# Two-layer transformer on one Trainium2 core: row-tiled maxima in layer 0's attention, one values block per unit in layer 1's

## The chip, the core and the metric

The kernel runs on one core of one Trainium2 chip. The core has five engines with a queue of their own each: PE (matmuls; its weight loads are listed as PEld), DVE (vector), ACT (scalar), POOL (GpSimd) and SP, which here only issues DMAs. They meet through semaphores. PE multiplies out of SBUF into PSUM, which has eight banks of 128 partitions x 512 fp32 values. The metric is the device time of one execution in microseconds. The kernel before takes 1522.89 us, the median of three runs (1521.58 to 1523.54).

## What is computed

Two layers, each an attention block and a feed-forward block with adaptive layer norms around them. The change touches the two softmax attentions. Layer 0's, cut to what matters (batch 2, sequence 1024, 16 query heads in 4 groups of 4 that share a key and value head, head dimension 64):

```python
q = (hidden_states @ Wq.T).reshape(B, S, NUM_HEADS, HEAD_DIM).transpose(0, 2, 1, 3)
k = (hidden_states @ Wk.T).reshape(B, S, NUM_KV_HEADS, HEAD_DIM).transpose(0, 2, 1, 3)
v = (hidden_states @ Wv.T).reshape(B, S, NUM_KV_HEADS, HEAD_DIM).transpose(0, 2, 1, 3)
...
scores = jnp.einsum('bhqd,bhkd->bhqk', q, k) * scale
scores = scores + causal[None, None]
probs = jax.nn.softmax(scores, axis=-1)
out = jnp.einsum('bhqk,bhkd->bhqd', probs, v)
return out.transpose(0, 2, 1, 3).reshape(B, S, NUM_HEADS * HEAD_DIM) @ Wo.T
```

The second attention, in the feed-forward block of layer 1, has the same form over the same 2048 tokens, with a head dimension of 8.

## The kernel before

The program is a chain of stages with a barrier between them. `stage_attention64` (layer 0) and `stage_attention8` (layer 1) work in the same way. A group g is one key head with its four query heads in one batch; there are 8. A group has 12 units, each 128 keys against up to 512 queries: four for the first half of the queries, eight for the second. On the diagonal a unit is only 384, 256 or 128 queries wide (`unit_lo`). For a unit PE makes transposed scores, ACT takes their exponential, POOL clears what lies above the diagonal, and two units later (`LAG`) PE multiplies the result with the values (`values`), out of weights of 32 columns on the four column quarters of the array.

The exponential needs each query's maximum before the scores, since it goes into the score matmul as a row (row 64 of `qB`, written by SP from `mT`). So a group's maxima are made while the group before is in its units: as max jobs, scores the other way round (queries on the partitions, keys along the bank), each reduced by DVE. Their matmuls stand in PE's queue as fills behind the scores.

Layer 0. Queries and keys are split: `proj` jobs (L500) give q and k from doubled weight columns, ACT rounds them to the high part (L708, L711), DVE subtracts it for the low part (L619, L624). A query head lies in `qA` with its high part on partitions 0 to 63 and its low part on 64 to 127; `kH` holds the key's high part twice. A score is two matmuls: L548 over 128 partitions, and L549 over 65 (the key's low part with `qB`, a copy of the query's high part that SP makes by DMA, plus the row of maxima). A max job (L510) is one matmul of 128 partitions for each head; with a key width of 128, 256, 384 or 512 a job takes 4, 2, 1 or 1 heads side by side in a bank, and a mask matmul in bf16 (L516) lies on the diagonal. There are 38 max jobs to a group, 22 with a mask. All jobs (proj, max, turn, fin) pass in one order through three banks (`JOB_BANKS`): job i waits until DVE is done with job i-3 (`w_free`). DVE takes them in the same order (`take`), with the copies of finished outputs (L655, L656), the reciprocals and the normalisation (L669) in fixed places between. A turn job (L522) transposes the maxima; fin (L528) is the output projection. `spread_over` lays the jobs over the units by weight (proj 3, others 1) and unit width, `parts` lays a unit's jobs and its three rounds of values over its score pieces. Where a unit opens an output (`opens`) no values stand behind its first score piece.

Layer 1. The 64 rows of a head's operands hold all split terms, so two heads lie on the halves of the array's rows (`row_tile`), as two matmuls into two banks. Scores (L983) go to three banks (`SCORE_BANKS`), so a score waits for the exponential of the score three before. A unit of 512 or 384 queries has four score jobs, a narrower one two. The max jobs (L956, masks L967 on the same row halves) use two pairs of banks. The values (L1009) are one bank.

```python
between = n >= LAG and len(jobs) == 4 and (n - LAG) % NU not in (0, 4)
```

Where `between` holds, a unit's values block stands between its second and its third score, otherwise behind the fourth. It holds for units 0, 1, 4, 5, 7, 8 and 9 of a group.

## Time and profile before

| | us |
|---|---|
| median of three runs | 1522.89 |
| the profiled execution, its time | 1521.91 |
| its span, first to last instruction | 1520.2 |
| layer 0's attention in it | about 39 to 646 |
| layer 1's attention in it | about 1021 to 1317 |
| PE busy, whole span | 1325.6 (87%) |
| DVE busy, whole span | 969.0 (64%) |
| ACT busy, whole span | 696.5 (46%) |

A row of the timeline has the start, the time to the end of the last instruction of the row, the engine, the line, the operation, what it writes and reads, and how many instructions are merged. Matmuls overlap: a matmul's recorded duration holds the filling and draining of the array, so what one costs the queue is the difference between its end and the end of the matmul before it. Where rows are added up here, that difference is meant. A values matmul of the order below is two instructions in the trace.

### The profile page before, as it was taken

How to read it: one execution, taken by the hardware profiler on the slowest of the kernel's cores; microseconds unless marked ns; L12 is line 12 of the kernel's file. 1: busy time of each engine (PE TensorE's matmuls, PEld its weight loads, DVE VectorE, ACT ScalarE, POOL GpSimd, SP SyncE). 2: the span in 40 equal slices, each digit the busy share in tenths (PEclk: the TensorE clock that was granted, in tenths of full speed). 3: DMA queues.
4: the chain of work that ended last, by engine and by line, in shares of the span. 5: the costliest groups of instructions: out<-in, count | busy, mean ns of one | idle time of the engine just before them, and what ended most of it. 6: DMA issues, size and time to landing. Idle time of an engine off the chain costs nothing. (4 is left out here: it accounts for less than half of the span.)

```text
span 1520.2 us, 21410 instructions
## 1 busy us (share of the span) xinstructions
PE 1325.6 (87%) x7772; PEld 762.8 (50%) x7772; DVE 969.0 (64%) x1750; ACT 696.5 (46%) x1319; POOL 112.6 (7%) x155
## 2 busy tenths in 40 slices
PE   4689999999999999868999967337989888889998
PEld 3344444444444444346888845313334333256886
DVE  4556545454546462177999966748767655357998
ACT  2242434333333433244666654412665556525664
POOL 0000000101010101000000000302111111020000
PEclk9799999999999999959999979656999888868999
DMA  3101202020201110006676610041212210102221
GB/s 104 40 15 34 49 15 63 8 58 15 52 15 43 29 29 16 14 15 144 146 154 153 146 24 1 2 100 54 47 48 49 53 40 20 43 21 79 78 102 28
DMA packets 51475, 81.61 MB, mean 54 GB/s; under 512 B 16748, under 2 KB 34452, under 8 KB 47444
## 3 DMA queue, kind: packets, MB, share of 16 engines
q1 hardware_dynamic: 51004, 79.40, 21.2%
q10 hardware_dynamic: 384, 1.05, 0.6%
q8 instruction: 55, 0.90, 0.2%
q14 instruction: 32, 0.26, 0.1%
HBM read 63.75 MB, written 5.68 MB: 46 GB/s over the span
## 5 line engine op out<-in xcount | busy, mean ns | idle before, releaser
L1345 PE MATMUL ps<-qA 128*128 128x512 f32 x960 | 252.3, 399 | 15.3 <-POOL qA L1455 10.9
L634 DVE TENSOR_REDUCE mraw<-ps 128x1 f32<-128x512 f32 (+3 forms) x304 | 186.8, 656 | 108.7 <-PE ps L516 60.2
L736 ACT ACTIVATE shared<-ps 128x512 f32<-128x512 f32 (+1 forms) x216 | 121.3, 566 | 261.4 <-PE ps L549 259.8
L1062 DVE TENSOR_REDUCE mraw<-ps 128x2 f32<-128x1024 f32 (+3 forms) x160 | 173.5, 1114 | 78.0 <-PE ps L967 52.3
L1117 ACT ACTIVATE shared<-ps 128x512 f32<-128x512 f32 (+2 forms) x320 | 155.7, 560 | 136.6 <-PE ps L983 136.0
L1345 PEld LDWEIGHTS ps<-qA 128*128 128x128 f32 x960 | 182.5, 192 | 62.9 <-POOL qA L1455 12.3
L548 PE MATMUL ps<-qA,kH 128*128 128x512 f32 (+3 forms) x384 | 165.9, 442 | 6.1 <-DMA qB<-mT 5.8
L548 PEld LDWEIGHTS ps<-qA,kH 128*128 128x128 f32 x384 | 72.9, 190 | 150.7 <-issue 62.6
L1409 ACT CAST qA<-shared 128x512 fp32r<-128x512 f32 x160 | 99.3, 621 | 88.6 <-DVE shared L1547 87.0
L1357 PE MATMUL ps<-qA,kH 128*128 128x512 f32 x480 | 136.3, 393 | 4.0 <-DVE qA L1471 4.0
L549 PE MATMUL ps<-qB,kL 65*128 65x512 f32 (+3 forms) x384 | 130.5, 350 | 0.0
L510 PE MATMUL ps<-kH,qA 128*128 128x512 f32 (+3 forms) x384 | 116.6, 369 | 9.4 <-DVE qA L624 7.8
L1471 DVE TENSOR_TENSOR qA<-shared,qA 128x512 fp32r<-128x512 f32 x160 | 110.0, 688 | 7.0 <-ACT qA L1409 2.0
L573 PE MATMUL ps<-shared 128*32 128x512 f32 (+3 forms) x1024 | 107.3, 509 | 0.0
L1547 DVE TENSOR_TENSOR shared<-shared 128x512 f32<-128x512 f32 x156 | 106.8, 685 | 0.0
L1357 PEld LDWEIGHTS ps<-qA,kH 128*128 128x128 f32 x480 | 90.2, 189 | 24.9 <-DVE qA L1471 6.1
L1009 PE MATMUL ps<-shared,VP 128*32 128x512 f32 (+3 forms) x768 | 93.9, 566 | 0.8 <-ACT oU L1104 0.4
L983 PE MATMUL ps<-qA,kH 64*128 64x512 f32 (+3 forms) x288 | 81.0, 461 | 14.9 <-ACT shared L1117 8.8
L956 PE MATMUL ps<-kL,qA 64*128 64x512 f32 (+3 forms) x288 | 70.3, 458 | 25.3 <-DMA kH<-qB 16.6
L736 ACT ACTIVATE rB<-ps 128x512 f32<-128x512 f32 x88 | 52.2, 599 | 87.7 <-PE ps L549 87.4
L510 PEld LDWEIGHTS ps<-kH,qA 128*128 128x128 f32 x384 | 69.8, 195 | 27.4 <-DVE qA L624 10.2
L983 PEld LDWEIGHTS ps<-qA,kH 64*128 64x128 f32 x288 | 37.7, 207 | 84.8 <-ACT shared L1117 57.8
(247 smaller groups left out, 1755.2 us busy)
## 6 DMA issues: line engine op xcount, KB each, us to landing
shared<-comb SPq DMA_DIRECT2D x92, 256.0 KB, 4.3
qB<-qA SPq DMA_DIRECT2D x16, 512.0 KB, 4.8
rB<-a0rec_dram SPq DMA_DIRECT2D x60, 128.0 KB, 2.8
shared<-comb SPq DMA_DIRECT2D x7, 1024.0 KB, 4.4
rB<-a1rec_dram SPq DMA_DIRECT2D x28, 128.0 KB, 2.7
e0wUp<-in_w SPq DMA_DIRECT2D x48, 64.0 KB, 4.5
qA<-q_split SPq DMA_DIRECT2D x24, 128.0 KB
q_split<-qA SPq DMA_DIRECT2D x4, 512.0 KB
```

Of the source, the lines that this page charges most:

```text
L510: ins = nc.tensor.matmul(bank[:, i * width:(i + 1) * width], k.qA[par][:, h0 + i, qt * P:(qt + 1) * P], k.kH[par][:, ch * 512:ch * 512 + w ...
L548: nc.tensor.matmul(out, k.kH[par][:, keys], k.qA[par][:, h, cols], start=True, stop=False)
L549: ins = nc.tensor.matmul(out, k.kL[par][0:hd + 1, keys], k.qB[par][0:hd + 1, h, cols], start=False, stop=True)
L573: nc.tensor.matmul(O[r][CT * at:CT * (at + 1), lo:512], v, probs(n)[:, 2 * r + i, lo:512], start=first, stop=last, skip_group_check=True)
L634: nc.vector.tensor_reduce(out[:, h0:h0 + n_h, qt % 4], src, AX, ALU.max).then_inc(w_free, 1)
L736: nc.scalar.activation(probs(n)[:, hs[0]:hs[-1] + 1, lo:512], src, ACT.Exp, scale=scale)\
L983: ins = nc.tensor.matmul(score_bank(s)[:, slot * w:(slot + 1) * w], kOne[g % 3][rows, kt * P:(kt + 1) * P], Q[g % 3][rows, h // 2, qc * 51 ...
L1062: nc.vector.tensor_reduce(out[:, :, js[0]:js[-1] + 1, qt % 4], src, AX, ALU.max).then_inc(x_free, 1)
L1117: nc.scalar.activation(dst, src, ACT.Exp, scale=scale).then_inc(p_done, 1)
L1345: ins = nc.tensor.matmul(bank[0:M, :], w[par][:, at:at + M], h[:, cols], start=(r == 0), stop=(r == 2))
L1357: ins = nc.tensor.matmul(acc(ch), w[par][:, m * D:(m + 1) * D], f[0:M, i % 2, :], start=(opens and r == 0), stop=(closing and r == 2), ski ...
L1471: nc.vector.tensor_tensor(fL[0:M, i % 2, :], k.hid[0:M, i % 2, :], fH[0:M, i % 2, :].bitcast(F32), ALU.subtract).then_inc(a_full, 1)
```

## The change

In layer 0 a query head of even number keeps its high part on partitions 0 to 63, and one of odd number has it on 64 to 127, the low part in the other half. ACT and DVE write them so (the same instructions, other partitions), and the DMA that copies the high parts to `qB` becomes two, one for the even and one for the odd heads. A max job now has heads of one parity and uses the high parts alone, 64 partitions; jobs come in pairs (`maxima`), an even and an odd one with alternating matmuls on the two halves of the array's rows, into two banks. Behind them stand both mask matmuls, still over 128 partitions. A pair waits until DVE has freed the bank of its second job. With key widths up to 256 a job holds two heads, otherwise one: 40 max jobs to a group in 20 pairs, 12 pairs with masks. A pair has weight 2 and is one fill. DVE reduces each job by itself.

In layer 1 `between` goes: the values always stand behind the unit's last score and fills.

```diff
--- before.py
+++ after.py
@@ -392,29 +392,31 @@
         out = []
         for qt in range(4 * qc, 4 * qc + 4):
             for ch in range(qc + 1):
-                n = 512 // keys_in(qt, ch)
-                out += [(qt, ch, h, n) for h in range(0, REP, n)]
+                if keys_in(qt, ch) <= 256:
+                    out += [(qt, ch, i, (i, i + 2)) for i in range(2)]
+                else:
+                    out += [(qt, ch, h % 2, (h,)) for h in range(REP)]
...
-        out += some[0:3] + [("proj", g, 1, 1)] + some[3:6] + [("proj", g, 1, 2)] + some[6:]
-        return out + more[0:3] + [("turn", g, 0, 0)] + more[3:]
+        out += some[0:2] + [("proj", g, 1, 1)] + some[2:4] + [("proj", g, 1, 2)] + some[4:]
+        return out + more[0:2] + [("turn", g, 0, 0)] + more[2:]
...
-        weights = [3 if job[0] == "proj" else 1 for job in jobs]
+        weights = [{"proj": 3, "max": 2}.get(job[0], 1) for job in jobs]
...
-        due[n] = list(range(len(JOBS), len(JOBS) + len(plan[n])))
-        JOBS += plan[n]
+        due[n] = []
+        for kind, g, qc, j in plan[n]:
+            both = [(kind, g, qc, j), (kind, g, qc, j + 1)] if kind == "max" else [(kind, g, qc, j)]
+            due[n].append(tuple(range(len(JOBS), len(JOBS) + len(both))))
+            JOBS += both
...
+                def maxima(pair):
+                    kind, g, qc, j = JOBS[pair[0]]
+                    par = g % 2
+                    if pair[1] >= JOB_BANKS:
+                        pe.wait_ge(w_free, pair[1] - JOB_BANKS + 1)
+                    if j == 0:
+                        pe.wait_ge(w_free, index["proj", g, qc, U - 1] + 1)
+                    qt, ch, _, evens = MAXES[qc][j]
+                    width = keys_in(qt, ch)
+                    diagonal = ch * 512 + width == (qt + 1) * P
+                    n_h = len(evens)
+                    for slot, h in enumerate(evens):
+                        for i in range(2):
+                            half = slice(i * hd, (i + 1) * hd)
+                            ins = nc.tensor.matmul(k.bank(pair[i] % JOB_BANKS)[:, slot * width:(slot + 1) * width],
+                                                   k.qA[par][half, h + i, qt * P:(qt + 1) * P],
+                                                   k.kH[par][half, ch * 512:ch * 512 + width], start=(slot == 0),
+                                                   stop=not diagonal, skip_group_check=True)
+                            if not diagonal and slot == n_h - 1:
+                                ins.then_inc(w_full, 1)
+                    if diagonal:
+                        for i in range(2):
+                            ends = k.bank(pair[i] % JOB_BANKS)[:, 0:n_h * width]\
+                                .rearrange("p (h w) -> p h w", w=width)[:, :, width - P:width]
+                            nc.tensor.matmul(ends, k.ident_bf[:, :], k.masks[:, 1:2, :].broadcast_to((P, n_h, P)),
+                                             start=False, stop=True, skip_group_check=True).then_inc(w_full, 1)
...
-                        pe.wait_ge(qb_ld[qc], 16 * (g + 1))
+                        pe.wait_ge(qb_ld[qc], 32 * (g + 1))
...
-                                ins = nc.vector.tensor_tensor(k.qA[par][hd:2 * hd, h, cols],
+                                ins = nc.vector.tensor_tensor(k.qA[par][(1 - i) * hd:(2 - i) * hd, h, cols],
                                                               bank[i * hd:(i + 1) * hd, :],
-                                                              k.qA[par][0:hd, h, cols].bitcast(F32), ALU.subtract)
+                                                              k.qA[par][i * hd:(i + 1) * hd, h, cols].bitcast(F32),
+                                                              ALU.subtract)
...
-                            ins = nc.scalar.copy(k.qA[par][0:hd, 2 * (j - 1) + i, cols], bank[i * hd:(i + 1) * hd, :])
+                            half = slice(i * hd, (i + 1) * hd)
+                            ins = nc.scalar.copy(k.qA[par][half, 2 * (j - 1) + i, cols], bank[half, :])
...
-                    sp.dma_start(k.qB[g % 2][0:hd, :, cols].bitcast(F32), k.qA[g % 2][0:hd, :, cols].bitcast(F32))\
-                        .then_inc(qb_ld[qc], 16)
+                    for i in range(2):
+                        sp.dma_start(k.qB[g % 2][0:hd, i::2, cols].bitcast(F32),
+                                     k.qA[g % 2][i * hd:(i + 1) * hd, i::2, cols].bitcast(F32)).then_inc(qb_ld[qc], 16)
...
@@ -1016,7 +1043,6 @@
                 for n in range(STEPS + LAG):
                     jobs = score_jobs(n) if n < STEPS else []
                     fills = list(due.get(n, []))
-                    between = n >= LAG and len(jobs) == 4 and (n - LAG) % NU not in (0, 4)
                     for at in range(max(len(jobs), 1)):
                         if at < len(jobs):
                             score_job(n, first_score[n] + at, *jobs[at])
@@ -1025,9 +1051,7 @@
                             for idx in fills[:share]:
                                 max_job(idx)
                             fills = fills[share:]
-                        if at == 1 and between:
-                            values(n - LAG)
-                    if n >= LAG and not between:
+                    if n >= LAG:
```

The order on PE from the last slot of a group's unit 5 (units are counted from 0) over the first two slots of its unit 6, layer 0 (L548 and L549 are scores, L510 maxima, L516 masks, L573 a round of values). Before:

```order
L548 MATMUL ps<-qA,kH 128x512
L549 MATMUL ps<-qB,kL 128x512
L510 MATMUL ps<-kH,qA 128x512
L516 MATMUL ps<-masks,ident_bf 128x128
L548 MATMUL ps<-qA,kH 128x512
L549 MATMUL ps<-qB,kL 128x512
L510 MATMUL ps<-kH,qA 128x512
L516 MATMUL ps<-masks,ident_bf 128x128
L548 MATMUL ps<-qA,kH 128x512
L549 MATMUL ps<-qB,kL 128x512
L510 MATMUL ps<-kH,qA 128x512 x2
L573 MATMUL ps<-shared 32x512 x4
```

Now (L568 and L569 are the scores, L510 the maxima, L520 the masks, L593 values):

```order
L568 MATMUL ps<-qA,kH 128x512
L569 MATMUL ps<-qB,kL 128x512
L510 MATMUL ps<-kH,qA 128x512 x2
L520 MATMUL ps<-masks,ident_bf 128x128 x2
L568 MATMUL ps<-qA,kH 128x512
L569 MATMUL ps<-qB,kL 128x512
L510 MATMUL ps<-kH,qA 128x512 x2
L568 MATMUL ps<-qA,kH 128x512
L569 MATMUL ps<-qB,kL 128x512
L510 MATMUL ps<-kH,qA 128x512 x2
L593 MATMUL ps<-shared 32x512 x4
```

The four max jobs of these three slots were one, one and two matmuls of full height. Now there are six, a pair of half height in each slot, and between the pair of one slot and that of the next stand only two score matmuls.

DVE at the same place (L624 the low parts of queries, L669 the normalisation, L634 the reductions, L655 and L656 the copies out of the output banks, L605 the fold of the maxima). Before:

```order
L669 TENSOR_TENSOR oU<-oU,rB 128x2x512
L634 TENSOR_REDUCE mraw<-ps 128x1 x4
L655 COPY S<-ps 128x512
L656 COPY oU<-ps 128x512
L634 TENSOR_REDUCE mraw<-ps 128x1
L605 COPY mmax<-mraw 128x16
L634 TENSOR_REDUCE mraw<-ps 128x1 x3
```

Now:

```order
L690 TENSOR_TENSOR oU<-oU,rB 128x2x512
L644 TENSOR_TENSOR qA<-ps,qA 64x512 x2
L655 TENSOR_REDUCE mraw<-ps 128x1 x4
L625 COPY mmax<-mraw 128x16
L676 COPY S<-ps 128x512
L677 COPY oU<-ps 128x512
L655 TENSOR_REDUCE mraw<-ps 128x1 x4
```

One projection's low parts now stand behind the normalisation, and behind the copies stand four reductions, those of unit 6's first two pairs, where before some of unit 6's came behind one and a fold.

Layer 1's attention on PE, from the block that is due in unit 5 to the block that is due in unit 7 (group 3) (L983 scores, L956 and L967 maxima and masks, L1009 values). Before:

```order
L1009 MATMUL ps<-shared,VP 32x128 x4
L983 MATMUL ps<-qA,kH 128x512 x2
L956 MATMUL ps<-kL,qA 128x256 x4
L967 MATMUL ps<-halves 128x2x128 x4
L983 MATMUL ps<-qA,kH 128x512 x2
L956 MATMUL ps<-kL,qA 128x512 x2
L983 MATMUL ps<-qA,kH 128x512 x2
L1009 MATMUL ps<-shared,VP 32x512 x4
L983 MATMUL ps<-qA,kH 128x512 x2
L956 MATMUL ps<-kL,qA 128x512 x2
L1009 MATMUL ps<-shared,VP 32x512 x4
```

Now (L1010 scores, L983 and L994 maxima and masks, L1036 values):

```order
L1036 MATMUL ps<-shared,VP 32x128 x4
L1010 MATMUL ps<-qA,kH 128x512 x2
L983 MATMUL ps<-kL,qA 128x512 x2
L1010 MATMUL ps<-qA,kH 128x512 x2
L1036 MATMUL ps<-shared,VP 32x512 x4
L1010 MATMUL ps<-qA,kH 128x512 x2
L983 MATMUL ps<-kL,qA 128x512 x2
L1010 MATMUL ps<-qA,kH 128x512 x2
L983 MATMUL ps<-kL,qA 128x384 x2
L994 MATMUL ps<-halves 128x128 x4
L1036 MATMUL ps<-shared,VP 32x512 x4
```

Between these blocks of values stood six and two score matmuls, and now four and four.

## Rows read from the trace of the kernel before

**Rows 1.** The page's first part: busy time of each engine, whole span.

```profile
PE 1325.6 (87%) x7772; PEld 762.8 (50%) x7772; DVE 969.0 (64%) x1750; ACT 696.5 (46%) x1319; POOL 112.6 (7%) x155
```

**Rows 2.** Windows of layer 0: length, busy and (count) of PE to POOL, clock, DMA.

```profile
340.00:440.00 100.00, 99.73 (x667) 45.76 (x665) 50.38 (x84) 36.80 (x65) 7.63 (x12) 1.00 0.11 26
```

**Rows 3.** Timeline of PE in layer 0: start, duration, instruction, count.

```profile
323.76 0.40 PE L510 MATMUL ps<-kH,qA 128*128 128x512 f32 x1
324.00 0.23 PE L516 MATMUL ps<-masks,ident_bf 128*128 128x128 bf16 x1
324.04 0.48 PE L548 MATMUL ps<-qA,kH 128*128 128x512 f32 x1
324.36 0.39 PE L549 MATMUL ps<-qB,kL 65*128 65x512 f32 x1
324.59 0.63 PE L510 MATMUL ps<-kH,qA 128*128 128x512 f32 x2
```

**Rows 4.** Groups by form, whole span: count, busy us, mean ns, idle before.

```profile
L510 PE MATMUL ps<-kH,qA 128*128 128x512 f32 x192 | 72.4, 423 | 4.1 <-DVE qA L624 2.8 <-DVE mraw L634 0.5
...
L516 PEld LDWEIGHTS ps<-masks,ident_bf 128*128 128x128 bf16 x176 | 17.1, 97 | 25.0 <-issue 19.6
```

**Rows 5.** Timeline of PE in layer 1's attention, around a turn.

```profile
1182.65 0.27 PE L945 MATMUL ps<-ident,mmax 128*16 128x128 f32 x1 [0.29 <-DVE mmax L1046]
1182.85 0.50 PE L956 MATMUL ps<-qA 64*128 64x512 f32 x2
...
1184.06 0.51 PE L983 MATMUL ps<-qA,kH 64*128 64x512 f32 x2
1184.40 0.40 PE L956 MATMUL ps<-qA 64*128 64x512 f32 x2
```

**Rows 6.** Timeline of PE in layer 0's experts, 32 rows then 128.

```profile
681.81 0.59 PE L1373 MATMUL ps<-y,sel 32*128 32x512 f32 x1
682.33 1.66 PE L1345 MATMUL ps<-qA 128*128 128x512 f32 x6
```

**Rows 7.** One line's instructions: L983's weight loads, ns min/median/max.

```profile
L983 PEld LDWEIGHTS ps<-qA,kH x288: 182/183/334, 1020.9 to 1313.9; 64*128 64x128 f32 x144
```

**Rows 8.** Timeline of DVE in layer 0, a group's units 4 to 6.

```profile
319.53 1.39 DVE L624 TENSOR_TENSOR qA<-ps,qA 64x512 fp32r<-64x512 f32 x2 [1.56 <-ACT qA L711]
320.95 1.23 DVE L669 TENSOR_TENSOR oU<-oU,rB 128x1024 f32<-128x1024 f32 x1
322.21 2.35 DVE L634 TENSOR_REDUCE mraw<-ps 128x1 f32<-128x384 f32 x4
324.48 0.68 DVE L655 COPY S<-ps 128x512 f32<-128x512 f32 x1
325.08 0.68 DVE L656 COPY oU<-ps 128x512 f32<-128x512 f32 x1
325.68 0.68 DVE L634 TENSOR_REDUCE mraw<-ps 128x1 f32<-128x512 f32 x1
```

**Rows 9.** Timeline of DVE in the opening of layer 0's attention.

```profile
46.00 6.33 DVE L634 TENSOR_REDUCE mraw<-ps 128x4 f32<-128x512 f32 x11 [1.05 <-PE ps L516]
```

**Rows 10.** Windows of layer 1's attention, columns as in rows 2.

```profile
1248.00:1252.00 4.00, 3.91 (x29) 1.48 (x21) 0.69 (x1) 1.31 (x3) 0.00 (x0) 0.63 0.03 6
```

**Rows 11.** Timeline of PE in that stretch.

```profile
1247.33 0.27 PE L945 MATMUL ps<-ident,mmax 128*16 128x128 f32 x1 [1.62 <-DVE mmax L1049]
```

**Rows 12.** Timeline of PE in layer 1's attention, units 6 and 7.

```profile
1159.56 0.84 PE L983 MATMUL ps<-qA,kH 64*128 64x512 f32 x2
...
1161.37 0.50 PE L983 MATMUL ps<-qA,kH 64*128 64x512 f32 x1 [0.45 <-ACT shared L1117]
1162.79 0.50 PE L983 MATMUL ps<-qA,kH 64*128 64x512 f32 x2
...
1165.06 1.07 PE L983 MATMUL ps<-qA,kH 64*128 64x512 f32 x2
```

**Rows 13.** Timeline of ACT in the same units.

```profile
1160.68 2.10 ACT L1117 ACTIVATE shared<-ps 128x512 f32<-128x512 f32 x4
```

More of the change, by code:

```diff
@@ L581, in values @@
                         ins.then_inc(pv_done, 1)
-                for idx in due[-1]:
-                    job(idx)
+                for group in due[-1]:
+                    job(group)
                 for n in range(STEPS + LAG):
@@ L818, in _ @@
                 load_out(1)
-                for idx in due[-1]:
-                    follow(idx)
+                for group in due[-1]:
+                    for idx in group:
+                        follow(idx)
                 for n in range(STEPS + LAG):
```

68 lines of the change are left out of this document (29 added, 39 removed).

## The prediction, as it was made

> **What bounds the kernel now.** I read the page's busy times first [rows 1]: PE is busy for 87% of the span, DVE for 64%, ACT for 46%. The two stages that change differ. In layer 0's attention the windows have PE at 99.7 of 100 us, at the full clock, and DVE and ACT at about half [rows 2]: there each nanosecond that PE's queue costs is one of the kernel's. In layer 1's attention PE waits now and then for the exponential or for a maximum [rows 11, 12], and the clock falls behind the long ones [rows 10]; an order of the same work can win or lose there. The other stages are not touched.
>
> **Layer 0, what the matmuls themselves save.** What a matmul costs in the queue is the distance from the end before it to its own. In rows 3 the score L549 ends at 324.75 and the two maxima of 512 keys behind it at 325.22: 0.23 us each, which is 512 columns in 0.213 us at 2.4 GHz and 0.02. By the same reckoning 384 and 256 columns are 0.18 and 0.13 (estimates), and for 128 I take 0.1, since the next weights are not loaded sooner. A group has 24 head matmuls at 512 and 8 at each of the other widths (192 at 512 in all [rows 4]). Do two matmuls on the two row halves cost as much as one? In layer 1 a pair L983 ends at 1184.57 and the pair L956 behind it at 1184.80 [rows 5]: 0.23 for two. So each pair saves one matmul: 96 x 0.23 = 22.1, 32 x 0.18 = 5.8, 32 x 0.13 = 4.2, 32 x 0.08 = 2.6, together 34.7 us. A mask of 128 columns ends 0.07 behind its maximum (324.16 to 324.23), and the 512 columns behind it take 0.29 instead of 0.23 [rows 3]. Masked jobs become pairs, so that tail of 0.06 comes 96 times instead of 176; with the mask columns about equal that is up to 3 us more. Saved: 38 us.
>
> **Layer 0, what the changes of tiling cost.** Scores, masks and projections stay at full height, so each pair is a change of the array's tiling. Two places show its price. The turn L945 (full height) ends at 1182.92 and the pair of 512 behind it at 1183.35 [rows 5]: 0.43 instead of 0.23. The matmul of 32 rows L1373 ends at 682.40 and the six of full height behind it at 683.99 [rows 6]: 1.59 where six times 0.23 are 1.39. That is 0.20 each way, near to one exposed weight load of 0.18 [rows 7]. For a mask the exposed load is the bf16 one of 0.097 [rows 4], so I put 0.107 there. Counted from the order of the new kernel: 155 changes from full height into a pair, 96 from a pair to its masks, 18 from a pair straight to a full-height matmul; 42 pairs go on to values, and that change was there before (full height to column quarters), so it is free. 173 x 0.20 + 96 x 0.107 = 34.6 + 10.3 = 45 us. The matmul work of layer 0 gets 7 us longer, not shorter. Bounds: if the mask's change costs 0.20 too, 9 more; if changes are hidden, all of the 38 us are won.
>
> The Trainium skill, page TensorEngine Tiling (Array Packing), section Key Properties, says that changing the tiling mode, not just the tile, drains the array. That rule speaks against this change; the trace agrees, with 0.20 us for a change, and a sum without it would be 38 us better off for layer 0.
>
> **Layer 0, waits for banks.** A job i waits for DVE to finish job i-3. A pair (i, i+1) waits for job i-2, the first of the pair before it, if pairs follow each other: PE can be one pair ahead at most, and both of its banks fill at once. In each of the six groups after the first whose loops carry maxima there is a place where DVE is behind: it works without a pause from 319.53 over the low parts (1.39), the normalisation (1.23), four reductions and the two copies (0.60 each, start to start) [rows 8]. In the new order two pairs stand in unit 6's first two slots with no values between. When the first of them ends, DVE is about at the fold, then has the copies, 1.2, and a reduction of 0.68: with the fold 2.05 us. PE has two scores (0.20 + 0.23 + 0.23) until it wants to issue the next pair. Its first matmul behind a wait takes 0.50 to its end, against 0.43 without. 2.05 + 0.05 - 0.66 + 0.07 = 1.5 us of stall. One pair earlier DVE has a projection's low parts and the normalisation to do first; the same reckoning gives some 0.7. The old order loses about 0.5 there (a wait for a reduction and one for the fold). So 1.7 us a group, times six: 10 us. PE is what waits, with the scores, values and thereby ACT queued behind it. In the opening DVE bounds: it did its eleven reductions in 6.33 us without a pause [rows 9]. Now DVE frees a bank, PE makes a pair in about 0.7, DVE has 0.6 of work left meanwhile: 0.1 to 0.2 lost at each of the 6 pairs ahead of the loop and of the 14 in the first four units, 3 us. Bounds of these waits: 0 if DVE is ahead, 20 if the smaller places of a group stall as well.
>
> The 16 further reductions are narrower (256 columns instead of 512) and are covered. ACT's and DVE's writes keep their sizes. The second copy DMA adds one issue on SP ahead of the maxima's rows, and a group's maxima come many units before its scores. Nothing for these; without that cover it would be 0.7 us at each of 16 places.
>
> **Layer 1.** A values block of 512 queries takes 1.0 us (the score ahead of one ends at 1161.87, the pair behind it at 1163.29, and a pair behind a change of tiling is 0.43 of that [rows 12]). Before, unit 6 had six score matmuls between two blocks. ACT needs about 0.5 us for each (four in 2.10, [rows 13]), PE waits 0.45 for one of them, and the unit takes 3.23 us (1159.56 to 1162.79), unit 7 with its block in the middle 2.27 (to 1165.06) [rows 12]. Now every unit has four scores between blocks: the fourth waits for the first exponential, which is done 0.50 + 0.04 + 0.60 = 1.14 behind the pair's start; another 0.50 and a block of 1.0 make some 2.7 us a unit. Units 0, 4 and 7 go from about 2.0 to 2.3 up to 2.6 to 2.9, units 1, 5, 8 and 9 (already held up at their second score) stay or gain 0.1, unit 6 falls to 2.7, and units 2 and 10, which follow on a pair of scores without a block between, lose up to 0.6 each. A group: about +1.6 and -2.0, so -0.4, times eight: -3 us. Both halves of that are soft: -8 to +8.
>
> **The sum.** 1521.9 (this execution, 1.0 below the median of the runs) + 7 + 10 + 3 - 3 = 1539 us. On the scale of the median it would be 1540; I keep 1539.
>
> **The rivals.** *Changes of tiling are hidden* (faster): a pair's weights are loaded under the full-height matmul ahead. Then the 38 us are won on PE, but PE comes sooner to DVE's busy stretches and loses perhaps 20 of them at the banks: 1521.9 - 38 + 20 + 3 - 3 = 1504. Against it stand both 0.20 us [rows 5, 6]. The Trainium skill, page TensorE: Matmul & The Clock Gate, section The mechanism, has PE pull a weight load for another row group ahead of running matmuls, which is what this rival needs; full height holds all row groups, so I give it 0.12. *DVE keeps ahead* (bank waits cost nothing): 1521.9 + 7 - 3 = 1526, chance 0.13, split between same and slower. *The clock falls*: a wait of 1.62 us in layer 1 [rows 11] was followed by a window at 0.63 [rows 10], so some 3 us at 1.2 instead of 2.4 GHz. If the 1.5 us stalls do that in six groups, at 2 to 3 us each, the time is 1539 + 15 = 1554; for it speaks the length of the wait, against it that PE here is full around it. Chance 0.15. *Layer 1 loses*: the 1.6 us a group come and the 2.0 don't: 1539 + 13 = 1552, chance 0.09. *The pair doesn't overlap in layer 0*: 35 more, 1574; rows 5 exclude it nearly, 0.02. The forecast, 1530 to 1549, has 0.49.
>
> The range, 1518 to 1560, leaves out the first rival, the last and a little at each end. A measurement of this kernel can tell 0.2%, about 3 us. The first rival and a small share of the forecast's lower end make faster 0.13; half of the second rival and what is left of that end make same 0.10; the rest is slower, 0.77.
>
> **What would show it.** Steps right: the first full-height score behind a pair ends 0.43 behind it, a pair of 512 behind a score 0.43; idle time of PE with a reduction of DVE as its releaser, above 1 us once a group in unit 6; layer 0's attention, about 607 us now, at about 627; layer 1's units near 2.7 and no unit 6 above 3. Wrong: layer 0's attention at 590 or less (changes hidden), or at 614 with no such waits; the clock below 1.00 in layer 0; layer 1's stage longer than 296 us.

## The result, and the profile after the change

The changed kernel takes 1561.18 us (median of 4 runs, 1556.65 to 1568.11) against 1523.21 of the kernel before in the same rounds: a ratio of 1.0255, 95% interval 1.0217 to 1.0294. The forecast was 1539 with a range of 1518 to 1560, so the direction was right and the size was not. The ratios leave out one run, at 1590.87 us, of the kernel with layer 1's part alone, whose mean granted clock was 0.80 against 0.92 in the others. The profiled execution took 1561.01 us with a span of 1559.3, against 1521.91 and 1520.2, so there are 39.1 us to explain.

TensorE's line of the page, beside [rows 1]: 18 us more busy for 16 more instructions, with 31 us less of weight loads.

```profile
PE 1344.0 (86%) x7788; PEld 731.5 (47%) x7788; DVE 972.9 (62%) x1766; ACT 695.6 (45%) x1319; POOL 112.6 (7%) x155
```

Where the time went is read by the starts of the score groups (every 48th first score matmul of layer 0, L548 before and L568 after; L983 and L1010 in layer 1):

| stretch | before | after | difference |
|---|---|---|---|
| start to layer 0's first score | 57.0 | 61.6 | +4.6 |
| group 0 | 92.1 | 103.1 | +11.0 |
| groups 1 to 6 | 429.2 | 458.4 | +29.2 |
| last group of layer 0 to layer 1's first score | 442.6 | 440.2 | -2.5 |
| layer 1, groups 0 to 6 | 262.2 | 258.7 | -3.5 |
| the rest | 237.1 | 237.3 | +0.3 |

(The differences are those of the unrounded times.) Of the first line 1.3 us lie ahead of anything that the change touches (the stage's first projection starts at 38.94 and at 40.27). The windows below are groups 0 and groups 1 to 6, first of before, then of after, with the columns of rows 2: length, then busy us of PE, PEld, DVE, ACT and POOL, each with its count, then the granted clock (1.00 is 2.4 GHz, 0.50 is 1.2 GHz), DMA share and GB/s.

```profile
57.00:149.10 92.10, 83.73 (x474) 41.76 (x474) 53.81 (x90) 30.86 (x54) 5.09 (x8) 0.95 0.12 28
149.10:578.30 429.20, 427.57 (x2860) 200.82 (x2856) 223.98 (x372) 170.16 (x300) 30.52 (x48) 1.00 0.14 34
```

```profile
61.60:164.70 103.10, 90.31 (x477) 37.74 (x477) 55.16 (x93) 30.82 (x54) 5.08 (x8) 0.84 0.10 25
164.70:623.10 458.40, 442.44 (x2873) 177.29 (x2869) 225.68 (x384) 169.78 (x300) 30.44 (x48) 0.97 0.12 31
```

In groups 1 to 6 PE's idle time grew from 1.6 to 16.0 us and its busy time by 14.9, while the clock, 1.00 throughout before, has a mean of 0.97. Nearly all the idle time has one releaser, the reductions of VectorE (waits of PE, 164 to 640 us; total us, times, longest):

```profile
PE ps L510 <- DVE mraw L655: 15.4, 24, 1.4
```

One place of each group holds most of it, the one that the prediction named. PE in group 2, units 5 and 6, after the change:

```profile
270.18 0.50 PE L510 MATMUL ps<-kH,qA 64*128 64x512 f32 x2
270.61 0.28 PE L520 MATMUL ps<-masks,ident_bf 128*128 128x128 bf16 x2
...
272.64 0.49 PE L510 MATMUL ps<-kH,qA 64*128 64x512 f32 x2 [0.72 <-DVE mraw L655]
...
274.08 0.49 PE L510 MATMUL ps<-kH,qA 64*128 64x512 f32 x2 [0.20 <-DVE mraw L655]
274.51 0.50 PE L568 MATMUL ps<-qA,kH 128*128 128x512 f32 x1
274.85 0.39 PE L569 MATMUL ps<-qB,kL 65*128 65x512 f32 x1
276.68 0.79 PE L510 MATMUL ps<-kH,qA 64*128 64x512 f32 x2 [1.44 <-DVE mraw L655]
277.40 1.93 PE L593 MATMUL ps<-shared 128*32 128x512 f32 x8
```

And VectorE there, which answers to [rows 8]:

```profile
271.89 1.29 DVE L655 TENSOR_REDUCE mraw<-ps 128x1 f32<-128x512 f32 x2
273.34 1.29 DVE L655 TENSOR_REDUCE mraw<-ps 128x1 f32<-128x512 f32 x2 [0.15 <-PE ps L520]
274.66 0.17 DVE L625 COPY mmax<-mraw 128x16 f32<-128x16 f32 x1
274.74 0.69 DVE L676 COPY S<-ps 128x512 f32<-128x512 f32 x1
275.34 0.68 DVE L677 COPY oU<-ps 128x512 f32<-128x512 f32 x1
275.94 1.28 DVE L655 TENSOR_REDUCE mraw<-ps 128x1 f32<-128x512 f32 x2
```

PE is through with its scores at 275.24 and wants the next pair; its bank comes free with the first reduction behind the fold and the two copies, at 276.6. That is the 1.44 us, forecast as 1.5. What follows was not in the sum. The last two rows of PE show a pair of 0.79 instead of 0.49 and a values block of 1.93, and the windows of the same stretch show why:

```profile
271.00:274.00 3.00, 2.17 (x16) 0.86 (x8) 2.80 (x6) 1.15 (x4) 0.00 (x0) 1.00 0.73 172
274.00:277.00 3.00, 1.47 (x6) 0.77 (x6) 2.96 (x7) 1.18 (x2) 0.00 (x0) 0.89 0.27 68
277.00:280.00 3.00, 3.00 (x12) 0.83 (x11) 1.51 (x3) 0.00 (x0) 0.00 (x0) 0.50 0.04 6
280.00:283.00 3.00, 3.00 (x12) 0.71 (x10) 0.28 (x1) 0.60 (x1) 0.00 (x0) 0.50 0.00 1
283.00:286.00 3.00, 3.00 (x16) 1.24 (x18) 0.79 (x3) 0.60 (x1) 0.00 (x0) 0.97 0.03 8
```

The clock is at 1.2 GHz while PE is busy without a gap. In each of the six groups it fell at this place, for 3.4 us in four of them and for 6.8 in two, 27.3 us in all. Unit 6 takes 12.3 us where the stretch is short and 13.4 or 13.7 where it is long, 8.84 before.

### The profile page after: what moved, and what is told of

It is laid out like the page before. It is cut to its first block and busy times, and to the rows that moved or that the text cites. A ratio compares the mean times of both kernels' runs of the same rounds, so it can differ in the third digit from the quotient of the medians.

```text
span 1559.3 us, 21474 instructions
## 1 busy us (share of the span) xinstructions
PE 1344.0 (86%) x7788; PEld 731.5 (47%) x7788; DVE 972.9 (62%) x1766; ACT 695.6 (45%) x1319; POOL 112.6 (7%) x155
## 5 line engine op out<-in xcount | busy, mean ns | idle before, releaser
L655 DVE TENSOR_REDUCE mraw<-ps 128x1 f32<-128x512 f32 (+3 forms) x320 | 188.4, 630 | 123.6 <-PE ps L520 68.4
L568 PE MATMUL ps<-qA,kH 128*128 128x512 f32 (+3 forms) x384 | 168.1, 448 | 5.0 <-DMA qB<-mT 4.7
L568 PEld LDWEIGHTS ps<-qA,kH 128*128 128x128 f32 x384 | 74.1, 193 | 161.2 <-issue 89.8
L569 PE MATMUL ps<-qB,kL 65*128 65x512 f32 (+3 forms) x384 | 132.7, 356 | 0.0
L593 PE MATMUL ps<-shared 128*32 128x512 f32 (+3 forms) x1024 | 119.3, 555 | 0.0
L510 PE MATMUL ps<-kH,qA 64*128 64x512 f32 (+3 forms) x384 | 82.8, 455 | 32.6 <-DVE mraw L655 25.2
L1010 PE MATMUL ps<-qA,kH 64*128 64x512 f32 (+3 forms) x288 | 82.5, 464 | 13.9 <-ACT shared L1141 7.6
L983 PE MATMUL ps<-kL,qA 64*128 64x512 f32 (+3 forms) x288 | 69.9, 465 | 25.7 <-DMA kH<-qB 16.6
L1036 PE MATMUL ps<-shared,VP 128*32 128x512 f32 (+3 forms) x768 | 91.0, 550 | 0.8 <-ACT oU L1128 0.5
L644 DVE TENSOR_TENSOR qA<-ps,qA 64x512 fp32r<-64x512 f32 x64 | 44.1, 689 | 61.9 <-ACT qA L735 61.4
L569 PEld LDWEIGHTS ps<-qB,kL 65*128 65x128 f32 x384 | 75.7, 197 | 4.3 <-issue 4.1
```

The costliest lines, as they stand in the source:

```text
L568: nc.tensor.matmul(out, k.kH[par][:, keys], k.qA[par][:, h, cols], start=True, stop=False)
L569: ins = nc.tensor.matmul(out, k.kL[par][0:hd + 1, keys], k.qB[par][0:hd + 1, h, cols], start=False, stop=True)
L593: nc.tensor.matmul(O[r][CT * at:CT * (at + 1), lo:512], v, probs(n)[:, 2 * r + i, lo:512], start=first, stop=last, skip_group_check=True)
L655: nc.vector.tensor_reduce(out[:, hs[0]:hs[-1] + 1:2, qt % 4], src, AX, ALU.max).then_inc(w_free, 1)
```

## The experiments

The first theory: layer 0's loss is three things, waits for banks, the clock that falls behind them, and an opening in which VectorE bounds; the halves of the rows cost and save about the same. The rival: the halves themselves cost it, through the changes of tiling. Where groups are given, they are the distances of the score groups in the profiled execution; "idle" is PE's idle time in groups 1 to 6.

**Layer 0's part alone.** The values of layer 1 stay between the scores, as before.

```diff
+                    between = n >= LAG and len(jobs) == 4 and (n - LAG) % NU not in (0, 4)
...
-                    if n >= LAG:
+                        if at == 1 and between:
+                            values(n - LAG)
+                    if n >= LAG and not between:
                         values(n - LAG)
```

> The change of layer 0 alone; layer 1's attention has its values in the middle of the unit again. The trace of the changed kernel has layer 1's stage 3.4 us shorter, so if that is the new order: 1564 us, 41 above the kernel before. If layer 1's gain in the trace was chance (its clock falls at other places), 1561.

Measured: 1564.12 us (1561.94 to 1566.61), ratio 1.0291 (1.0261 to 1.0321). Groups 1 to 6 took 76.0 to 77.3 us, group 0 105.3, layer 1's groups 0 to 6 260.0. The loss is layer 0's.

**Layer 1's part alone**, in the kernel before: the same lines the other way round.

```diff
-                    between = n >= LAG and len(jobs) == 4 and (n - LAG) % NU not in (0, 4)
...
-                        if at == 1 and between:
-                            values(n - LAG)
-                    if n >= LAG and not between:
+                    if n >= LAG:
                         values(n - LAG)
```

> The change of layer 1 alone. If the new order saves 3 us: 1520, at 3 below the kernel before, and unit 6 of a group below 3 us where the clock is full. If its gain was chance: 1523, or above it if the fourth score's wait for the first exponential is not won back.

Measured: 1512.39 us (median of six runs, five of them at 1507.09 to 1514.94), ratio 0.9935 (0.9896 to 0.9973), so 10 us faster than before, where the prediction had 3. The windows over layer 1's groups 0 to 6, of before and then of this kernel:

```profile
1020.90:1283.10 262.20, 224.53 (x1734) 100.98 (x1734) 184.38 (x194) 140.93 (x293) 41.01 (x59) 0.85 0.21 51
```

```profile
1020.80:1273.80 253.00, 215.81 (x1736) 97.52 (x1736) 185.05 (x194) 140.75 (x293) 40.94 (x59) 0.89 0.21 53
```

PE's idle time is nearly the same, 37.7 and 37.2 us. 8.7 of the 9.2 us are busy time, with 56.1 us at 1.2 GHz instead of 76.4: 20.3 us less at half speed are worth up to 10. The idle time is in smaller pieces where the block of values moved: there were 19 waits of 0.3 to 0.6 us before and there are 13 now, while those over 0.6 us stay (14 with 23.5 us before, 15 with 24.7 now). That this keeps the clock up is likely and not shown. Unit 6, which answers to [rows 12]:

```profile
1159.79 0.40 PE L956 MATMUL ps<-kL,qA 64*128 64x512 f32 x2
1160.03 0.39 PE L983 MATMUL ps<-qA,kH 64*128 64x512 f32 x1
1160.69 0.49 PE L983 MATMUL ps<-qA,kH 64*128 64x512 f32 x1 [0.28 <-ACT shared L1114]
...
1161.42 1.07 PE L1009 MATMUL ps<-shared,VP 128*32 128x512 f32 x8
1162.42 0.50 PE L983 MATMUL ps<-qA,kH 64*128 64x512 f32 x2
...
1163.66 0.49 PE L983 MATMUL ps<-qA,kH 64*128 64x512 f32 x1 [0.16 <-ACT shared L1114]
```

The wait of 0.45 us of [rows 12] is one of 0.28 here. The units are the ones forecast (2.69 us for unit 6 of that group, to 1162.42, and 2.90 for the next), so the order does what was said, and the sum left out what the clock gives back.

**Full height, with the same pairs and waits.** A maximum runs over all 128 rows, as before; nothing else differs from the change (the low parts on the other rows are multiplied too).

```diff
-                            half = slice(i * hd, (i + 1) * hd)
...
-                                                   k.qA[par][half, h + i, qt * P:(qt + 1) * P],
-                                                   k.kH[par][half, ch * 512:ch * 512 + width], start=(slot == 0),
+                                                   k.qA[par][:, h + i, qt * P:(qt + 1) * P],
+                                                   k.kH[par][:, ch * 512:ch * 512 + width], start=(slot == 0),
```

> The changed kernel with the same pairs, order and waits, but each maximum matmul over all 128 partitions as before (high and low parts). No change of tiling is left; the pair's two matmuls are one after the other. Theory one, waits for banks and the clock they bring down are most of the loss: only the matmul work changes, 45 us of tiling changes go and 35 of matmuls come back, so 1545 to 1553, with unit 6 of a group still above 11 us. Theory two, the tiling changes are the loss: 1535 or less.

Measured: 1545.71 us (1536.53 to 1550.82), ratio 1.015 (1.0109 to 1.0191), 15 us less than the change though its matmuls work longer. The profiled execution, at 1550.82, is the slowest of its four. The waits are all there:

```profile
PE ps L509 <- DVE mraw L654: 16.3, 24, 1.4
```

```profile
273.94 0.73 PE L509 MATMUL ps<-kH,qA 128*128 128x512 f32 x2 [1.40 <-DVE mraw L654]
```

but the clock fell behind them in two groups out of six, 6.8 us in all instead of 27.3; the other four take 74.7 us. PE was no busier there: of the 5 us up to the end of the longest wait it was busy for 2.62 us, and for 2.65 in the change. In the opening, too, the clock comes back sooner. Windows of the change, then of this kernel:

```profile
72.00:78.00 6.00, 4.44 (x18) 2.30 (x16) 4.12 (x8) 0.98 (x2) 0.64 (x1) 0.50 0.13 33
78.00:84.00 6.00, 5.22 (x19) 2.78 (x19) 4.37 (x7) 0.98 (x2) 0.63 (x1) 0.50 0.00 0
84.00:90.00 6.00, 4.70 (x18) 2.71 (x16) 4.05 (x8) 1.19 (x2) 0.63 (x1) 0.50 0.00 0
```

```profile
72.00:78.00 6.00, 5.64 (x17) 4.08 (x18) 3.58 (x7) 1.09 (x2) 0.63 (x1) 0.50 0.41 100
78.00:84.00 6.00, 4.41 (x19) 2.54 (x17) 5.61 (x10) 1.47 (x3) 0.63 (x1) 0.95 0.00 0
84.00:90.00 6.00, 4.69 (x24) 2.94 (x24) 5.20 (x9) 1.20 (x2) 0.63 (x1) 1.00 0.00 0
```

With full height the clock comes back at about 79 us, and with the halves it stays at 1.2 GHz for 23.9 us, to about 95. This was a second theory, new here: matmuls on half of the rows keep the clock down where there are waits. The two openings don't show it by themselves. PE is busy about as long in both, 14.4 and 14.7 us of these 18, but not in the 6 us ahead of the return, 5.64 against 4.44: full-height matmuls also leave PE less idle there. And the stretch at 1.2 GHz before this one, ahead of and behind the first score, is the longer one with full height, 23.9 against 17.1 us. Up to the end of group 0 they add up to 34.1 against 47.8.

**The jobs of units 2 and 6 one slot later**, in the changed kernel.

```diff
-            out.append((hs, fills[len(fills) * i // k:len(fills) * (i + 1) // k], rounds))
+            share = lambda j: fills[len(fills) * j // k:len(fills) * (j + 1) // k]
+            if m >= 0 and opens and k == 4:
+                mine = [[], share(0), share(1), share(2) + share(3)][i]
+            else:
+                mine = share(i)
+            out.append((hs, mine, rounds))
```

> The changed kernel, with the fills of units 2 and 6 (where no values stand behind the first score) one slot later, so that PE has a round of values between two pairs there. Work, tiling changes and job order stay. Theory one: the wait of 1.44 us and the clock's fall behind it go, unit 6 takes 9 to 9.5 us instead of 12.3 to 13.7, six groups: 1538 to 1545. Theory two: 1558 to 1562.

Measured: 1532.84 us (1530.89 to 1535.24), ratio 1.0091 (1.0063 to 1.0118): 28 us less than the change by one slot in two units, and more than was expected. Of the 30.1 us between the profiled executions 21.6 are groups 1 to 6 (458.4 to 436.8; unit 6 takes 9.1 us) and 5.0 are layer 1, which this edit doesn't touch. The wait of 1.44 us is gone, the earlier one of 0.71 stays, and no group has a stretch at 1.2 GHz:

```profile
162.30:599.10 436.80, 429.21 (x2873) 175.49 (x2869) 225.81 (x384) 169.16 (x300) 30.44 (x48) 1.00 0.12 33
```

With the clock at 1.00 here and before, the busy times can be compared: 429.2 against 427.6 us. The pairs on the halves, changes of tiling and all, cost 1.6 us in these six groups.

**One wait for each job, at full height.** The two jobs of a pair follow each other, each behind the wait for its own bank, each with its mask behind it.

```diff
-                    if pair[1] >= JOB_BANKS:
-                        pe.wait_ge(w_free, pair[1] - JOB_BANKS + 1)
...
+                    for i, idx in enumerate(pair):
...
+                        if idx >= JOB_BANKS:
+                            pe.wait_ge(w_free, idx - JOB_BANKS + 1)
```

> The changed kernel with maxima matmuls of full height (128 partitions, as in the kernel before) and with the same slots for the pairs, but each job of a pair waits for its own bank only, directly in front of its matmuls, and its mask follows it directly. Against full height with the pair's wait (1545.71 us, groups 1 to 6 at 74.7, first score group 99.3) only the wait and the order inside a pair differ. If the pair's common wait for two banks is what costs: groups 1 to 6 at 71.5 to 72, first group 92 to 94 us, no 1.2 GHz stretch in them, total 1513 to 1520 us. If the slots of the pairs (two jobs where one stood, one slot earlier) cost by themselves: groups stay over 74 us and the total over 1538 us.

Measured: 1532.27 us (1528.41 to 1536.85), ratio 1.007 (1.0047 to 1.0092). Both halves of the expectation missed: groups 1 to 6 took 73.8 us (75.3 in the two where the clock fell). The waits of 0.78 and 0.20 are gone, but one of 1.39 stays in unit 6. So that one is not the price of waiting for two banks at once; it comes of four jobs standing where VectorE is behind. The opening is another matter: layer 0's first score came at 57.7 us and group 0 took 95.1. From the stage's first projection to the end of group 0 that is 113.1 us, where full height with the pair's wait took 122.7, the change 124.4 and the kernel before 110.2 (112.5 in the run with layer 1's part alone, whose layer 0 is the same). The pair's common wait is most of the opening's loss.

**Half of the reductions' work left out**, in the changed kernel and, as a control, in the kernel before: VectorE's maxima of layer 0 read the first half of each head's keys only.

```diff
-                        src = bank[:, 0:len(hs) * width].rearrange("p (h w) -> p h w", w=width)
+                        src = bank[:, 0:len(hs) * width].rearrange("p (h w) -> p h w", w=width)[:, :, 0:width // 2]
```

> The changed kernel, with VectorE's maxima reductions of layer 0 reading only the first half of each head's keys: half of that reduction's work is left out, TensorE's work, its order and its waits are those of the changed kernel. If VectorE's speed sets when the banks come free, and the clock falls because of the waits for them: waits of 1.4 us shrink to under 0.5, no 1.2 GHz stretch in groups 1 to 6, groups at 72.7 us, first group near 95, total 1528 to 1532 us. If the two-row-half matmuls themselves (their tiling changes, or fewer active rows) cost the rest or bring the clock down: groups over 75 us, total over 1553 us.

> The control for the half reduction: the kernel before with the same half of the reduction's work left out. If TensorE's order there hardly waits for the reductions: groups at 71.0 to 71.5 us, total 1514 to 1520 us. If it gains as much as the changed kernel does (over 20 us), VectorE's pace bounded layer 0 before too, and the half reduction tells nothing of the pairs.

Measured: 1538.22 us (1536.51 to 1539.01), ratio 1.0106 (1.0081 to 1.0131), for the changed kernel, 23 us less than with the whole reductions, and 1510.77 (1508.03 to 1514.0), ratio 0.9926 (0.9903 to 0.9949), for the kernel before, 11 us less than its 1521.74. Of the 22.1 us between the changed kernel's profiled executions 6.5 are layer 1, which the edit doesn't touch; 13.2 are groups 1 to 6. In the kernel before those give 3.4 (71.54 to 70.97 a group), the stretch ahead of them 4.7 and the one from the last group to layer 1 3.0, which is scatter: that stretch takes 442.6 us in the profiled execution of before and 439.3 in the one with layer 1's part alone, on the same instructions. So VectorE's pace bounds the changed kernel's layer 0 more than the old one's. The waits did not vanish as expected: one of 0.45 and one of 0.90 us are left in each group,

```profile
PE ps L510 <- DVE mraw L655: 8.1, 12, 0.9
```

and behind these the clock still fell in three of the six groups (17.1 us at 1.2 GHz). In the other three a group takes 73.0 us, near the 72.7 expected.

**The later slot in the old order**, with layer 1's part: both diffs from above on the kernel before.

> The kernel before in layer 0 with the maxima jobs of units 2 and 6 one slot later, and layer 1's values as one block behind a unit's scores as in the change. If the waits for banks in unit 6 of the old order (0.5 us a group) can be taken away by this: 1508 to 1511 us, groups 1 to 6 of layer 0 at 71.0 us. If they only move to the next unit: 1512 us as with the layer 1 part alone (1512.39), groups at 71.5 us.

Measured: 1517.13 us (1512.97 to 1521.53), ratio 0.9969 (0.9949 to 0.9989). The rival was right, and more: groups 1 to 6 went from 71.54 to 71.93 us, with a wait of 0.44 us in front of each group's output projection where the old slots have one of 0.12 in front of the transposed maxima. The slot that helps the pairs hurts the old order.

**Full height in group 0 alone**, else the changed kernel: a test of the second theory in the opening.

```diff
-                            half = slice(i * hd, (i + 1) * hd)
+                            half = slice(0, P) if g == 0 else slice(i * hd, (i + 1) * hd)
```

> The changed kernel with maxima matmuls of full height in group 0 alone (before and in the first group of scores); the order, the waits and the other groups are the change's. In the changed kernel TensorE ran at 1.2 GHz for 23.9 us from 71.5 us on, with full height everywhere for 6.8 us. If matmuls on 64 rows keep the clock down in the opening: the 1.2 GHz stretch from about 71 us on is under 8 us, the first group 98 to 100 us instead of 103.1, the total 1556 to 1558 us. If the waits for banks alone keep it down (they stay): first group 102 to 104 us, total 1560 to 1563 us.

Measured: 1554.86 us (1551.14 to 1562.67), ratio 1.0234 (1.0187 to 1.0281). Group 0 took 99.4 us, with 6.8 us at 1.2 GHz from 71.9 us on instead of 23.9, so it was 3.7 us shorter. But the way from the stage's first projection to the first score grew from 21.3 to 23.5 us, so the opening as a whole gained 1.6 us, and two executions of the change's layer 0 differ by more than that in it (124.4 us, and 126.7 with layer 0's part alone). The sign is the one of the second theory, the size small. The total can't show it: of the 9.9 us between the profiled executions 6.5 are layer 1, which the edit doesn't touch.

**Full height and the later slot:** the diffs of those two runs together.

> The changed kernel with the maxima jobs of units 2 and 6 one slot later (as in the run before with that edit, 1532.84 us) and with maxima matmuls of full height in all groups. If the 1.25 us by which groups 1 to 6 of that run exceed the old 71.5 are the tiling changes less the matmul time saved: groups 1 to 6 at 71.5 to 71.9 us, first group 98 to 99, total 1520 to 1524 us. If the halves bring a net gain in the steady part: groups over 73 us, total over 1533 us.

Measured: 1531.78 us (1528.33 to 1536.34), ratio 1.007 (1.0051 to 1.009). Groups 1 to 6 took 73.09 us, over the bound that was set for a net gain by the halves, but the windows give another reason.

```profile
159.90:598.40 438.50, 430.16 (x2873) 195.81 (x2869) 225.78 (x384) 169.12 (x300) 30.46 (x48) 1.00 0.12 33
```

Against the halves in the same order, PE is busy for 430.2 instead of 429.2 us: all the halving, with its changes of tiling, gains 1 us in six groups. Of the 1.25 us a group by which the run with the later slot and the halves exceeds the old 71.54, 1.0 is idle time and 0.26 work; here, of 1.55 us, 1.1 is idle time (8.3 us in the six groups against 1.6). So it is mostly not the tiling. Group 0 took 97.8 us against 101.9 with the halves, and the first score came 1.2 us later behind the first projection.

**The later slot, and group 0 with full height and one wait for each job.** `maxima_alone` is the function of the run with single waits.

```diff
-                        maxima(group)
+                        (maxima_alone if JOBS[group[0]][1] == 0 else maxima)(group)
```

> The kernel with the jobs of units 2 and 6 one slot later (halves of the rows, pairs in one wait), but in group 0 alone full height and one wait for each job. If the opening's extra is the pair's common wait plus the halves at 1.2 GHz: first group 92 to 96 us instead of 101.9, groups 1 to 6 at 72.8 us, total 1524 to 1528 us. If it is the doubled number of jobs in a slot: first group over 99 us, total over 1530 us.

Measured: 1521.04 us (1516.34 to 1530.31), ratio 0.9999 (0.9973 to 1.0025): no different from the kernel before, and under the 1524 to 1528 expected; the groups are as expected. Layer 0's first score came at 57.6 us and group 0 took 95.9; before, 57.0 and 92.1. The opening's loss, 15.6 us in the change and 13.2 with the later slot alone, shrinks to 4.4 us by what is done to one group out of eight. By the run with single waits in all groups it is the waits more than the height that do it.

**Both cures everywhere:** full height with one wait for each job, and the jobs one slot later, the diffs of those two runs together.

> Both cures at once: maxima matmuls of full height with one wait for each job (1532.27 us alone, PE idle 1.6 us a group, of it one wait of 1.39 in unit 6) and the jobs of units 2 and 6 one slot later (1532.84 us with the halves, PE idle 1.3 us a group, of it one wait of 0.71 one pair earlier). If these are two separate waits, each cure takes its own: PE idle under 0.6 us a group, groups 1 to 6 at 71.7 to 72.1 us, first group 92 to 95 us, total 1510 to 1517 us. If the later slot only turns one wait into the other: idle over 1.2 us, groups 72.8 to 73.5, total over 1520 us.

Measured: 1514.66 us (1512.67 to 1516.53), ratio 0.9953 (0.9936 to 0.997).

```profile
57.40:148.90 91.50, 82.97 (x477) 41.05 (x477) 53.68 (x93) 30.85 (x54) 5.08 (x8) 0.97 0.11 28
148.90:581.80 432.90, 431.79 (x2872) 199.15 (x2868) 223.56 (x384) 169.29 (x300) 30.44 (x48) 1.00 0.13 33
```

The two waits are separate: with both cures 1.1 us of idle time are left in six groups, and group 0 is as fast as before. Layer 0 is then within 3.7 us of its old time in the six groups, now busy time (431.8 against 427.6 us) and not idle; what is left of the change there is its slots and its 16 further jobs. The gain over before is layer 1's. Of all the kernels here that do the whole work layer 1's part alone is the fastest by its median, 1512.39 us, and it beats both kernels of the case; its interval and that of the last run overlap.

## Why the prediction was wrong in size

**Changes of tiling: right by the piece, a little high in the sum.** The pair behind a score ends 0.43 us behind it (the score ahead of 270.18 in the timeline ends at 270.25, the pair at 270.68), its masks 0.21 behind that; both are as put down. The sum was +7 us for eight groups. The busy times at full clock give +1.6 for six, so about +2 for eight. Halving alone, against full height in the same order, gives -1 us in six groups, where the sum had 35 saved and 45 lost in eight. (The text is off by small amounts elsewhere: it takes 0.1 us for 128 columns and then sums with 0.08, which is 0.6 us in all, and the sum for layer 0 without the changes of tiling would be 45 us better off, not 38.) A part of the difference can be read: a pair that stands behind a wait takes 0.49 us (272.64 above) against 0.73 for two at full height (273.94 in that run), so its change of tiling is paid in the idle time; 18 such waits of six groups in the run with the later slot are 3.6 us at 0.20 each, an estimate from these rows. The Trainium skill, page TensorEngine Tiling (Array Packing), section Key Properties, has each change of tiling mode drain the array; the 0.20 us of a change agree with it. The saving of one matmul in two is eaten by the changes.

**Waits for banks: right place, right size of the largest, sum low.** The waits measured 1.44 us against 1.5, and 0.72 against 0.7. Left out were waits of 0.20 and 0.22 us, and the old order's waits were put at 0.5 a group where the trace's idle time of PE is 0.27 a group. Idle time grew by 14.3 us in groups 1 to 6, not by 10.

**The step that failed: the clock.** The text had it as a rival, "The clock falls", at 0.15 and 15 us, and named against it "that PE here is full around it". That was the wrong argument. PE was busy for 99.7 of 100 us [rows 2] and the change left it so but for the waits; the clock fell in every group all the same. So the sum put the clock at nothing. The text also named a clock below 1.00 in layer 0 as a sign of being wrong, and it is 0.97. The measured 27.3 us at 1.2 GHz cost what is left of the 29.2 us, 29.2 - 14.3 - 1.6 = 13.3 us (half of 27.3 is 13.7), and with those 1539 becomes 1552. The rows of the experiments show what stood ahead of a fall. With waits of 0.7 to 0.8 and of 0.2 to 0.3 us and no longer one it came in none of 18 groups (the later slot with the halves, with full height, and with group 0 treated). With 0.78, 0.20 and 1.40 at full height it came in two of six, and with 1.39, with one of 0.15 ahead of it, in two of six. With 0.72, 0.20 and 1.44 and the halves it came in 18 of 18 (the change, layer 0's part alone, and full height in group 0 alone). So the waits bring it, and with the halves it came every time. That the halves add to it rests on this 18 of 18 against 2 of 6, at the same waits and with PE as busy ahead of them, but the 2 of 6 are one execution, and why the rows should matter is open. The Trainium skill, page TensorE: Matmul & The Clock Gate, Part 1, says that the throttled state is the default and that activity releases it; the return to 2.4 GHz behind 6 us of PE without a gap (277 to 283 in the windows above) agrees.

**The opening: 3 us forecast, 14.3 measured** (4.6 + 11.0, less the 1.3 of an earlier stage). The step that failed is the reckoning of "0.1 to 0.2 lost at each of the 6 pairs" on VectorE. It had PE make a pair in about 0.7 us. The reductions that ran without a pause in [rows 9] now stand in pairs with gaps:

```profile
47.11 0.76 DVE L655 TENSOR_REDUCE mraw<-ps 128x2 f32<-128x256 f32 x2 [0.84 <-PE ps L520]
48.74 1.29 DVE L655 TENSOR_REDUCE mraw<-ps 128x2 f32<-128x512 f32 x2 [0.87 <-PE ps L520]
50.44 1.02 DVE L655 TENSOR_REDUCE mraw<-ps 128x1 f32<-128x384 f32 x2 [0.40 <-PE ps L520]
```

VectorE waits for PE and PE for VectorE by turns (PE's pairs at 49.49, 51.05 and 52.61 wait 0.54 to 0.57 each), PE goes down to 1.2 GHz, the pairs take 0.7 to 0.8 us and 1.0 to 1.3 with their masks, and VectorE's gaps are 0.4 to 0.9 where 0.1 to 0.2 were reckoned. The pair's common wait makes them take turns: with one wait for each job, at full height in all groups, 9.6 us of the opening went. The time at 1.2 GHz up to the end of group 0 rose from 17.1 to 47.8 us. The experiments part the 15.6 us of both lines of the table: with the later slot alone 60.5 us to the first score and 101.9 for group 0; with full height as well 62.0 and 97.8, in sum 2.5 less; with one wait for each job in addition, both in group 0 alone, 57.6 and 95.9 us. What the last 4 us of group 0 are was not tried by itself. Two executions of the old layer 0 have 92.1 and 94.1 there, so half of them can be scatter; where all groups had single waits at full height and the later slot, they were gone, and group 1's maxima, which stand in group 0's units, were treated too.

**Layer 1: right mechanism, too small.** -3 was forecast within -8 to +8, and layer 1's part alone gave -10. The unit times were worked out at full clock, and the gain of the run alone is in the clock. In the profiled execution of the change layer 1 gave only 3.5 us. Of the eleven profiled kernels with the new order eight take 252.2 to 253.7 us for these seven groups, with 55.9 to 64.4 us of them at 1.2 GHz, and three, the change among them, 257.1 to 258.7, with 67.5 to 76.7 us; with the old order the three kernels take 260.0 to 262.3. PE's idle time is 35.6 to 37.8 us in all with the new order. So the -3.5 lies at the upper end of a scatter that goes with the clock, and what sets the clock there was not tried.

**The others.** *Changes hidden* (1504) is excluded by the 0.43 us. *DVE keeps ahead* (1526) is excluded by the waits. *Layer 1 loses* is excluded by its run alone; its price is off too, since the sum without the 2.0 us a group is 16 us higher and not 13, 1555. *The pair doesn't overlap* (1574) is excluded by the 0.43 us as well. The 2.5 us which the change is shorter between the last group and layer 1's first score are within the scatter of that stretch (442.6 and 439.3 us in two executions of the old layer 0); no instruction there differs.

The sum with the measured terms, in the profiled execution: 1521.9 + 1.6 (work) + 14.3 (idle) + 13.3 (clock) + 15.6 (opening, with the earlier stage) - 2.5 - 3.5 + 0.3 = 1561.0. The clock's term is the remainder of groups 1 to 6, so the sum closes by construction.

## What to carry to other kernels

A wait is priced with what follows it: look for how long the engine waited at other places and whether the clock fell behind, and if one such place exists, put its cost into the sum and not among the rivals. When two jobs are joined under one wait, ask whether producer and consumer now take turns, and how many jobs stand at the place where the consumer is behind; the common wait was worth 10 us in the opening here, and one slot's shift 22 us in six groups. Halving the rows of a matmul between full-height neighbours saved next to nothing here (1 us in six groups), where each half-height pair brought a change of tiling both ways.

## What the runs showed of the hardware

- The clock of a stream busy for 96 to 98% of its time (99.6% before) fell to 1.2 GHz for 3.4 or 6.8 us at a wait of 1.4 us: in two of six groups where only one of 0.15 us stood ahead of it, at full height; in two of six at full height and in all of eighteen with the pairs on half of the rows, where waits of 0.7 to 0.8 and 0.2 us did. It fell in three of six groups at waits of 0.45 and 0.90 us with the halves. At waits of 0.7 to 0.8 us and shorter it didn't fall (0 of 18).
- Up to the end of group 0, in the same order and with the same waits in the code, the time at 1.2 GHz was 47.8 and 54.6 us with matmuls on half of the rows and 34.1 and 37.5 us with matmuls on all of them. In the 6 us ahead of the return of the clock PE was also busier with full height, 5.64 against 4.44 us, so the rows alone are not shown to be the cause.
- A change of the array's rows costs 0.20 us in front of a pair of 512 columns; the two halves run side by side, so that pair and change together took 0.43 us, where two matmuls of full height took 0.48 in the run with full height and the later slot. Behind a wait the change adds nothing: 0.49 us for the pair against 0.73 for the two at full height.
